# Bucket-sum places loaded one word at a time, and a counting sort of nine chunks instead of eight

## What is computed

```python
src = edge_index[0]
sums = jax.ops.segment_sum(edge_attr, src, num_segments=n)
counts = jax.ops.segment_sum(jnp.ones((edge_attr.shape[0],), edge_attr.dtype), src, num_segments=n)
edge_attr_agg = sums / jnp.maximum(counts, 1.0)[:, None]
```

## Time and profile before

| | us |
|---|---|
| three executions | 2975.58, 2984.27, 2985.07 |
| their median | 2984.27 |
| the profiled execution | 2979.5 |
| its span | 2977.7 |
| first put on GpSimd | 27.91 |
| bucket sums on TensorE | 679.35 to 1270.6 |

### The profile page before, as it was taken

One profiled execution on the slowest core, in us unless ns is written; L12 is line 12 of the kernel. 1 busy time (PEld: TensorE's weight loads), 2 busy tenths in 40 slices (PEclk: granted clock), 3 DMA queues, 4 the chain that ended last, 5 costly groups with the idle time before them and its releaser, 6 DMA issues.

```text
span 2977.7 us, 48133 instructions
## 1 busy us (share of the span) xinstructions
PE 2175.2 (73%) x14401; PEld 2005.6 (67%) x14402; DVE 1892.7 (64%) x2801; ACT 970.0 (33%) x2710; POOL 2039.3 (68%) x1727
## 2 busy tenths in 40 slices
PE   0000037778888888799699995888988775699998
PEld 0000026657888888777599994777777664699998
DVE  8979987742323222356577676975555447698897
ACT  0000002220111111123366663555554441455553
POOL 5777777777777777401066663777777773678886
PEclk9999997885555555689899997999998888799999
DMA  6543345555444445312112223776777775423230
GB/s 211 151 122 90 97 109 152 150 150 130 115 119 116 110 115 132 95 60 74 54 32 57 57 59 100 192 195 190 189 193 194 190 194 156 112 67 91 64 98 32
DMA packets 332219, 358.48 MB, mean 120 GB/s; under 512 B 200434, under 2 KB 239216, under 8 KB 331828
## 3 DMA queue, kind: packets, MB, share of 16 engines
q1 hardware_dynamic: 210475, 196.63, 23.0%
q0 software_dynamic: 95744, 93.58, 13.7%
q10 hardware_dynamic: 25859, 66.47, 7.1%
HBM read 241.40 MB, written 122.94 MB: 122 GB/s over the span
## 4 chain that ended last, share of the span: by engine, by line
POOL 37%; PE 32%; issue 15%; DVE 12%; DMA 2%; ACT 1%; POOLq 0%; DVEq 0%; SPq 0%; ACTq 0%
POOL sorted L1155 30%; POOL mid L1231 6%; PE ps L2294 3%; PE ps L2394 3%; PE ps L2413 2%; PE ps L2272 2%; PE ps L2349 2%; PE ps L2351 2%; PE ps L2350 2%; PE ps L2371 2%; PE ps L2372 2%; PE ps L2370 2%; DVE yb L2125 1%; PE ps L2337 1%; PE ps L2540 1%
## 5 line engine op out<-in xcount | busy, mean ns | idle before, releaser
L1231 POOL DMA_INDIRECT mid<-h_rows,idx_a x400 | 486.0, 1215 | 131.0 <-issue 124.9
L2245 PE MATMUL ps<-big 128*128 128x65 f32 (+1 forms) x2380 | 493.1, 406 | 101.3 <-issue 82.2
L2245 PEld LDWEIGHTS ps<-big 128*128 128x128 f32 x2380 | 488.6, 320 | 107.2 <-issue 107.2
L1155 POOL DMA_INDIRECT sorted<-yb,idx_a x200 | 238.0, 1190 | 84.1 <-issue 60.7
L1583 DVE TENSOR_TENSOR big<-ps,big 128x1792 f32<-128x1792 f32 x85 | 171.6, 2020 | 176.4 <-PE ps L2245 163.9
L1164 POOL TENSOR_TENSOR rstd<-var,neg_half 125x2 f32<-125x2 f32 (+1 forms) x75 | 64.3, 858 | 316.0 <-DVE var L1638 315.8
L1155 POOL DMA_INDIRECT sorted<-wk,idx_a x200 | 238.3, 1191 | 61.0 <-issue 61.0
L1155 POOL DMA_INDIRECT sorted<-mid,idx_b x200 | 237.5, 1187 | 61.0 <-issue 60.6
L1155 POOL DMA_INDIRECT sorted<-xh,idx_b x200 | 237.4, 1187 | 61.0 <-issue 61.0
L1824 DVE TENSOR_TENSOR mid<-ps,xTg 128x256 bf16<-128x256 f32 (+1 forms) x245 | 122.3, 499 | 218.6 <-PE ps L2404 216.2
L1826 DVE TENSOR_TENSOR hT<-ps,mid 128x608 bf16<-128x608 f32 (+3 forms) x245 | 254.8, 1040 | 0.1
(11 more groups left out here) (381 smaller groups left out, 6312.0 us busy)
## 6 DMA issues: line engine op xcount, KB each, us to landing
h_in_r<-h_parts SPq DMA_DIRECT2D x245, 256.0 KB
big<-sorted ACTq DMA_DIRECT2D x85, 469.0 KB, 4.1
sorted<-hT SPq DMA_DIRECT2D x73, 469.0 KB, 7.4
mid<-in_L_ffn_w SPq DMA_DIRECT2D x16, 1024.0 KB
hid_x<-hT ACTq DMA_DIRECT2D x25, 500.0 KB
mid<-hid_x SPq DMA_DIRECT2D x25, 500.0 KB
h_parts<-h_part_r SPq DMA_DIRECT2D x24, 480.0 KB
mid<-h_rows,idx_a POOLq DMA_INDIRECT x400, 4.6
```

Source lines behind the costliest of these rows:

```text
L1155: nc.gpsimd.indirect_dma_start(sorted_rows[c], bass.IndirectOffsetOnAxis(to_row[k][:, i:i + 1], 0), va[k][:, i, :], None).then_inc(s_put[k ...
L1231: nc.gpsimd.indirect_dma_start(mg4[:, s, i, :], None, h_rows, bass.IndirectOffsetOnAxis(idx4[:, s, i:i + 1], 0)).then_inc(s_gk[s], 16)
L2245: i_ = mm(banks[:, bass.ds(o_, w)], node_hot[:, s % 2, i, :], rows[:, i, 0:w], start=False, stop=True, skip_group_check=True)
```

## The change

`CB` gets nine chunks: the last 20 blocks are 8, 8 and 4 instead of 12 and 8. `ZSEM`, the semaphore that each chunk's zero fill counts on, gets a ninth entry, the same as the two before it. All other counts follow: `CG` is then 7, 12, 9, 9, 9, 18, 9, 9, 7, `NGA` 89 instead of 85, `WIDE_AT` 82 instead of 76. In `bucket_sums` the load of 28 words before every fourth group goes; instead a group loads its first word before its waits, and each further word just before the two products that come ahead of it.

```diff
--- before.py
+++ after.py
@@ -15,7 +15,7 @@
 SLOTS = 1000
 ST = SLOTS // P
 HB = B // 2
-CB = (4, 12, 8, 8, 8, 20, 12, 8)
+CB = (4, 12, 8, 8, 8, 20, 8, 8, 4)
 CFIRST = tuple(sum(CB[:c]) for c in range(len(CB)))
 CLAST = tuple(CFIRST[c] + CB[c] - 1 for c in range(len(CB)))
 GA = 14
@@ -52,7 +52,6 @@
 MADD = tuple((r, c) for r in range(len(RANGES)) for c in RANGES[r][1])
 WP = GA // 2
 NV = 4
-LW = 4
 SW = 100
 WIDE_AT = NGA - CG[-1]
 NS = 4
@@ -64,7 +63,7 @@
 ROW_PARTS = (slice(0, 120), slice(120, P))
 PW = 16 * len(ROW_PARTS)
 CT = ET // G
-ZSEM = (0, 1, 2, 2, 3, 3, 4, 4)
+ZSEM = (0, 1, 2, 2, 3, 3, 4, 4, 4)
 HW = EB // 2
 MEAN, RSTD, PROB = range(D, D + 3)
 XW = D + 3
@@ -2224,14 +2223,12 @@
                 mm(ps[:, k, :], z[0:1, 0:BR], z[0:1, 0:512], start=True, stop=True)
             banks = ps[:, :, :].rearrange("p k n -> p (k n)")
 
-            held = []
-
             def bucket_sums(g, s=None):
                 s = g % NS if s is None else s
-                if s % LW == 0:
-                    n = min(LW, NGA - g) if isinstance(g, int) else LW
-                    _, held[:] = nc.values_load_multi_w_load_instructions(place_words[0:1, bass.ds(g * WP, n * WP)], engines=[pe.engine])
-                pairs = held[s % LW * WP:(s % LW + 1) * WP]
+                def places(j):
+                    return pe.value_load(place_words[0:1, bass.ds(g * WP + j, 1)])
+
+                pair = places(0)
                 wide = isinstance(g, int) and g >= WIDE_AT
                 if wide:
                     pe.wait_ge(s_wide, WIDE + g - WIDE_AT + 1)
@@ -2240,7 +2237,9 @@
                 w, rows = (SW, sums_in[:, (g - WIDE_AT) % 2]) if wide else (CW, rows2[:, s])
                 pe.wait_ge(s_hot2, g + 1)
                 for i in range(GA):
-                    o_ = pe.snap(pairs[i // 2] >> 12 if i % 2 else pairs[i // 2] & 4095)
+                    if i % 2 == 0:
+                        now, pair = pair, places(i // 2 + 1) if i < GA - 2 else None
+                    o_ = pe.snap(now >> 12 if i % 2 else now & 4095)
                     o_ = nc.s_assert_within(o_, 0, 7 * 512, skip_runtime_bounds_check_because="a bucket's place is at most that of the last")
                     i_ = mm(banks[:, bass.ds(o_, w)], node_hot[:, s % 2, i, :], rows[:, i, 0:w], start=False, stop=True, skip_group_check=True)
                 i_.then_inc(s_a2, 1)
```

## The result

Over six runs of each, the changed kernel took 2994.27 us (2990.32 to 2997.3) and the kernel before 2980.53 us (2975.58 to 2985.07): a ratio of 1.0047, with a 95% interval of 1.0037 to 1.0057. It is slower by 13.7 us, more than the 0.3% that a measurement of this kernel can tell. The forecast was 6 us more, counted as no change.

What follows compares the result with a forecast made beforehand. GpSimd's puts were taken as the bound, so only work behind the last put counts: bucket sums end at 1276.6 for 1270.6, 6 us more. Forecast 2988, between 2985.5 and 2990.3; range 2980 to 2994, wider 2973 to 3010.

Steps and rivals of the forecast that it cites:

- The bound: GpSimd's puts of edges' rows: 14.92 us a block, ending at 1222.6; only what follows the last put moves the end.
- More groups, VectorE: 85 to 89 groups, 82 before the last chunk; positions work on VectorE up to 8 us longer, costed at nothing.
- The price of a word: TensorE's one-word loads: 0.34 us each with the step; a loop group 6.1 us, a fixed-number group 5.2.
- The eighth chunk: Groups 73 to 81: first load at 1176.3, first product 1182.8, nine groups at 6.08 us, done at 1237.5.
- Landing 4.2: Eighth chunk's first load of sorted rows: 4.2 us to landing, before 2.0 for one-hots and 0.3 to the product.
- The last chunk: Seven wide groups: start 2.1 us after the eighth chunk, at 1239.6, 37.0 us long, ending 1276.6 against 1270.6.
- The slower one: Words dearer than 0.37 us: at 0.40, 12 us more; at 0.48, 41 us more, 3025. Chance 0.32.
- The faster one: Word loads hidden beside the issue of products: 7 us less, or 15 less with the full clock. Chance 0.12.
- The 0.6 us a word: A word price of 0.6 us from the rule on loads, given 0.03 of the slower rival's 0.32 chance.
- The clock: TensorE's granted clock stays at 0.50 in the narrow products; gaps are not what keeps it low.
- the faster rival's last case: Hidden words and unbroken products at full clock: eighth chunk done by 1230, end 1255, 15 us less, 2969.
- The sum: One path to the end of the bucket sums: 1276.6 against 1270.6, 6 us more; predicted time 2988 us.

Runs made afterwards that it cites:

- seven_words: The changed kernel with a group's seven words in one load ahead of the group's waits: 2983.95 us, 1.0018 of the kernel before.
- words_only: The kernel before with its eight chunks kept and only the words loaded one by one: 2986.26 us, 1.0029 of the kernel before.
- seven_both: The changed kernel with ScalarE's sorted-row loads before its copies, SyncE's burst held until 80 groups are summed, seven words per load: 2976.90 us, 0.9995 of before.
- sync_later: The changed kernel with SyncE's hidden-row loads and kept-end stores held until 80 groups are multiplied: 2986.67 us, 1.0035 of the kernel before.

## Why the prediction was right or wrong

**The bound.** Right: the puts kept their rhythm and only what stands behind the last one moved the end.

**More groups, VectorE.** Right where it matters. The positions' last chunk boundary came at 398.98 us for 393.28, 5.7 us (forecast up to 8), and the bucket sums began 1.8 us later. The last put came 0.45 us later, so of this at most 0.45 us reached the path.

**The price of a word.** Right. How many words each load of the earlier trace rows has stands in the kernel: one at L2489 and at L802, seven at L2233 for group 84, which stands alone, and 28 for the others; so 1.702 us are 0.243 a word and 7.281 are 0.260. A word's load was put at 0.309 us and measured at 0.303, and seven wide groups took 36.8 us for 37.0. The step to the next instruction was put at 0.03 and wasn't measured by itself, nor was the 0.35 for the waits at a loop group's head, which stands in no row; a wide group of the changed kernel, 5.2 to 5.4 us behind the first two, bears out the sum of 5.2. That a load one pair ahead still costs its whole time was the author's assumption, which no row showed; the runs agree with it in the wide groups, 5.2 to 5.4 us for seven single words where the products alone are 3.36. (A pair of products has three register instructions on the sequencer, not two: five wide groups of 70 products show 69 FUSED_REGOPS and 34 ALU_OP. The 0.37 us for a pair is a time per pair and stays.) In the eighth chunk nine groups took 56.2 us for 54.7: 6.25 a group, not 6.08, 1.5 us more.

**The eighth chunk.** Here the forecast failed, in one term: "Landing 4.2". The issue was nearly right (1176.3 forecast, 1176.87 measured), and the landing took 10.9 us. Group 73 began at 1190.78 for 1182.8, 8.0 us late: 6.7 of them are the landing, 0.6 the issue, and 0.7 the way from the one-hots' start to the first product (3.0 us for 2.3). Of the 9.2 us by which the end was later than forecast (1285.8 for 1276.6), 8.0 are this late start, 1.5 the narrow groups, and 0.3 came back in the rest. The earlier trace rows gave the means to see it: the median of all loads is 4.2 but the longest 9.3, and the median over the 20 us in question was 9.0 already in the kernel before. A median over the whole program was put on a step whose time is known. The range 2973 to 3010 held the result, but that is luck: it was made wide for the price of words and has nothing in it for this. The narrower range of 2980 to 2994, 2 to 9 us more, was missed by the 13.7.

**The last chunk.** Right: 2.0 us from the last narrow group to the first wide one (2.1 forecast), 36.8 for the seven groups (37.0). The 3.1 us of a group at the full clock and the clock in GHz are shown by no run: in `seven_words` the granted clock was 0.50 from 1246.33 to 1249.00 and 1.00 from 1254.95 to 1258.30, where a group's 28 records took 3.36 us, and its first two groups took 8.21 together, 1.5 more than twice that.

**The rivals.** The slower one as written (words dearer than 0.37) didn't come about; the kernel was slower through a mechanism that stood in none of the cases. (At 0.40 a word the prediction's own 1.1 us for each 0.01 gives some 1283.2, not 1282.9.) The faster one (words hidden) is refuted by `words_only`: nine wide groups with single words took 7 us longer, with nothing else changed. Its sum has a slip: seven groups at 3.1 and 0.8 for the clock are 22.5 us, and the 24.9 that it adds goes with 3.36 and a gap of 0.2 a group. The 0.6 us a word, to which 0.03 of the slower rival's chance is given, is shown by no run: the 623 loads of one word in the changed kernel took 0.303 us in the median and 1.052 at most.

**The clock.** Right. In the changed kernel stretches of 36.79 and 19.11 us without a gap stayed at a granted clock of 0.50; in this stage it rose only in the wide products, to 1.00 from 1281.00 to 1285.00. The windows of after, 100 us of narrow products and all the wide ones:

```profile
1050.00:1150.00 100.00, 96.52 (x428) 93.10 (x427) 30.10 (x16) 13.04 (x66) 79.54 (x68) 0.50 0.45 121
1249.00:1285.80 36.80, 32.65 (x196) 26.65 (x196) 10.26 (x6) 5.64 (x6) 0.00 (x0) 0.94 0.16 50
```

TensorE was busy 96.5% of those 100 us and the clock stayed low. What keeps it low there, no run tests; unbroken narrow products didn't bring the full clock, as the faster rival's last case has them do.

**The sum.** The parts interact, so a sum over them alone would have been far off; the forecast went along one path instead, which suits this: words alone 8.8, chunks alone 34.6, together 13.7 us.

## What to carry to other kernels

When a change makes an engine wait for a transfer that used to be early, take that transfer's duration from the same stretch of the trace, with whatever other queues move there, not from the median of its line. Ask of each queue what stands ahead of the transfer that has become urgent: here exchanging two blocks of ScalarE's loop took the ratio from 1.0047 on one chip to 1.0004 on another, each against the kernel before on its own. And a wait that ties a burst to another engine's progress must be looked at again whenever that engine gets faster, since the burst moves with it.

## What the runs showed of the hardware

- Loads of words on TensorE's sequencer took their time out of open products even when loaded a pair ahead: 5.2 to 5.4 us a wide group with seven single words (the changed kernel, `words_only`), 4.0 to 4.6 with one load of seven (`seven_words`), of which the products are 3.36. One load of seven took 1.70 us, one single 0.303.
- In three runs the longest of these loads stood where the DMA engines were busy: 1.05 us for one word in the changed kernel, with a DMA share of 1.03 in the view of 697.80 to 698.90 where it ran, 2.07 in `words_only`, with 0.98, and 6.40 for seven in `seven_both`, with 0.93, where SyncE's burst and ScalarE's loads met. The share alone doesn't tell it: one word of the changed kernel took 0.77 us at a share of 0.34, and the other seven of `seven_both` 5.36 at 0.42. In `sync_later`, where only the burst was moved, the words of group 81 went from 0.30 to 0.97 us in the median. What in the burst slows them isn't shown.
- The same burst slowed the landing of a load of 469 KB: the first of four issued together landed in 10.9 us beside it (the changed kernel) and in 3.4 without it (`sync_later`).
- The same kernel before took 2977 to 2981 us on three occasions and 3083.58 on another chip, 3.5% more, with a ratio of 1.0078 where the first gave 1.0047 for the changed kernel. What makes that chip slow wasn't found out.
